# Sparse experts: first-layer weights by a DMA for each tile, the gate's clamp on ScalarE, the norm scale on the turned rows

## The chip, the cores and the metric

The kernel runs on one core of one Trainium2 chip. The metric is the device time of one execution in microseconds (us). A core has five engines with instruction queues of their own: TensorE (PE in the profile; PEld is its loading of weights), VectorE (DVE), ScalarE (ACT), GpSimd (POOL) and SyncE (SP). They meet by semaphores. DMAs are issued from a queue (here SP's, ACT's and GpSimd's) and carried out by 16 DMA engines that all queues share.

## What is computed

Two blocks on x of 16 sequences, 512 tokens, 128 features. The first has a linear recurrence per channel and eight experts of one layer; the second a linear attention with 16 heads and eight experts of two layers, of which each token takes the best two. The change touches only the last of these:

```
def _swiglu(h):
    x_glu = minimum(h[..., ::2], 7.0)
    x_lin = clip(h[..., 1::2], -7.0, 7.0)
    return x_glu * sigmoid(1.702 * x_glu) * (x_lin + 1.0)

t = x * rsqrt(mean(x * x) + EPS) * norm_scale            # 8192 tokens of 128
top_v, top_i = top_k(t @ gate_w + gate_b, 2)
w = zeros.at[token, top_i].set(softmax(top_v))
for w1, b1, w2, b2, we in experts:                       # w1 128x512, w2 256x128
    acc = acc + we * (_swiglu(t @ w1 + b1) @ w2 + b2)
return x + acc
```

## The kernel before

The kernel has three phases. The last, from about 350 us on, holds the second attention, the sparse experts and the sum. Each engine has one block of code in which its instructions stand in their order.

**The attention** goes over 16 sequences (B = 16) in a software pipeline written out by hand: in round n each engine does one step of several sequences. It also norms each sequence's rows, chooses two experts for every token, and scatters each token's row (128 numbers and 4 more, PAY = 132) twice into `rows_of` in DRAM, sorted by expert: `send`, L1479, on GpSimd. At the start of this phase SP loads what the experts need: `w1` of all eight experts (2 MB, L1402) with their biases (L1405) into `w1b1`, which lies in the room of the tile `xg` (so the profile calls it xg), 516 columns for each expert: 512 of weights and 4 of biases. In rounds 7 to 10 ScalarE multiplies the weights by the norm scale `ns`, two experts at a time (`scaled_weights`, L1674). VectorE adds 1 to the biases of the linear half (`numbers`, L1990).

**The plan.** After the last sequence VectorE works out which expert and which rows of `rows_of` each of BT = 72 tiles has (L2036 to L2060). A tile is 256 rows of one expert. The first rows are numbers in `meta`; the experts of 8 tiles are packed into one number in `packs`. An engine loads such a number into a register (`row`, L1335; `packed`, L1340) and takes the expert of a tile out of it by a shift and a mask (`expert`).

**The sparse experts** go over 72 tiles, nine passes of V = 8. For tile v:
- SP loads the 256 rows (132 KB) into slot v % 8 of `xt`, which lies in `kvb` (L1432). It waits until the rows of tile v-8 are turned and their places are worked out.
- TensorE turns the rows (L2417) into bank v % 2. ScalarE copies them to `x_t`, which lies in `qd` (L1725).
- ScalarE copies the expert's 516 columns into `w1c[v % 2]`, which lies in `ex` or `lg` (`own_weights`, L1732). A register gives the column.
- TensorE does the first layer (L2432), 4 matmuls of 128x128 weights with 256 rows, seen as 8 records since fp32 takes two. Their results lie in two banks, gate first.
- VectorE adds the bias and clamps the gate, `glu` (L2104), and the linear half, `lin` (L2109); both lie in `qk`. ScalarE does the gelu of the gate in `gs`, which lies in `nrm` (L1747). VectorE makes the product `act_t`, which lies in `f_t` (L2095).
- Two steps later TensorE adds the bias (L2446) and does the second layer (L2451). ScalarE weighs the result into `yw`, which lies in `h` or `gx` (L1756). Another step later GpSimd scatters it in two DMAs into `parts` in DRAM (L1504).
- For every fourth tile VectorE works out places and weights of four tiles (L2075 to L2088).

The orders are: TensorE turn(v+1), first layer(v), second layer(v-2). ScalarE turned(v+1), own_weights(v+1), gelu(v), weighted(v-2). VectorE gate(v), linear(v), product(v), at times places. After the last tile SP reads `parts` (L1445), VectorE adds it to `x_tok`, and ACT's queue writes the output.

## Time and profile before

| | before |
|---|---|
| runs | 1069.51 us median of 3 (1068.09 to 1073.88) |
| span of the profiled execution | 1003.5 us |
| PE busy | 837.3 us, 83% |
| PEld busy | 645.8 us, 64% |
| DVE busy | 827.6 us, 82% |
| ACT busy | 619.4 us, 62% |
| POOL busy | 563.5 us, 56% |
| DMA | 84.47 MB, mean 84 GB/s |

The span runs from the first to the last instruction; the 66.0 us between it and the median of the runs lie outside. The share of busy time is a mean over stages with different limits. The slices of the page show these (each digit is the busy share in tenths of one fortieth of the span, 25.1 us; PEclk is the clock that TensorE was granted, in tenths of full speed):

```profile
PE   6887972899999579999999999994149999999900
DVE  3987769899997586789999999997638888888848
ACT  3475128899983474587787767746236666666600
POOL 1221018568760534336888888887727676767720
PEclk9999895799999879999999999996569999999955
DMA  5230541333233050000111111111243333233168
```

The last phase starts at slice 15. The sparse experts are slices 30 to 38, the sum is slices 39 and 40.

### The profile page before, as it was taken

Reading aid. Unit: us, or ns where it says so; the run is one execution under the profiler, and the core shown is the slowest. Engines: PE = TensorE matmul, PEld = TensorE weight load, DVE = VectorE, ACT = ScalarE, POOL = GpSimd, SP = SyncE. Lnnn points to the kernel's source line nnn. Section 1 sums busy time; section 2 is a strip of 40 time slices with the busy share of each in tenths; the row PEclk is TensorE's granted clock in tenths of the full one; section 3 lists DMA queues with packets and bytes.
Section 4 is the critical chain, followed back from the end, with each engine's and each line's share of the span. In section 5 each row is a group of like instructions: output and inputs, shape, how many; then the busy total and the mean of one; then the engine's idle time right before and its main releaser. Section 6 shows DMA issues by size and latency. Waiting matters only on the chain.

```text
span 1003.5 us, 22806 instructions
## 1 busy us (share of the span) xinstructions
PE 837.3 (83%) x7439; PEld 645.8 (64%) x7439; DVE 827.6 (82%) x2204; ACT 619.4 (62%) x1669; POOL 563.5 (56%) x573
## 2 busy tenths in 40 slices
PE   6887972899999579999999999994149999999900
PEld 6854652444454268888888888883038888889800
DVE  3987769899997586789999999997638888888848
ACT  3475128899983474587787767746236666666600
POOL 1221018568760534336888888887727676767720
PEclk9999895799999879999999999996569999999955
DMA  5230541333233050000111111111243333233168
GB/s 153 82 90 1 143 134 46 130 105 138 90 127 127 9 145 19 2 10 26 37 44 34 37 36 45 36 37 47 95 122 94 89 90 89 89 95 97 54 227 296
DMA packets 74479, 84.47 MB, mean 84 GB/s; under 512 B 14254, under 2 KB 64361, under 8 KB 72188
## 3 DMA queue, kind: packets, MB, share of 16 engines
q1 hardware_dynamic: 56492, 60.06, 19.7%
q0 software_dynamic: 8704, 18.11, 5.4%
q10 hardware_dynamic: 9168, 4.87, 1.6%
q8 instruction: 61, 1.00, 0.4%
q14 instruction: 54, 0.44, 0.2%
HBM read 59.33 MB, written 23.67 MB: 83 GB/s over the span
## 4 chain that ended last, share of the span: by engine, by line
PE 51%; DVE 6%; DMA 2%; issue 2%; POOL 1%; SPq 1%; ACT 1%; POOLq 0%; DVEq 0%; ACTq 0%
PE ps L2432 13%; PE ps L2194 11%; PE ps L2451 6%; PE ps L2210 3%; PE ps L2272 2%; PE ps L2185 2%; PE ps L2417 2%; PE ps L2331 2%; PE ps L2311 2%; PE ps L2205 1%; POOL rows_of L1479 1%; PE ps L2156 1%; PE ps L2171 1%; PE ps L2259 1%; DVE x_tok L2128 1%
## 5 line engine op out<-in xcount | busy, mean ns | idle before, releaser
L1470 POOL TENSOR_TENSOR kvb<-qk,v 128x1024 f32<-128x1024 f32 x64 | 126.7, 1984 | 74.7 <-DVE qk L1854 50.4
L1479 POOL DMA_INDIRECT rows_of<-payb,posu x128 | 144.1, 1126 | 40.6 <-issue 27.0
L1115 PE MATMUL ps<-masked,ew 128*128 128x512 f32 x256 | 129.9, 623 | 4.2 <-DVE masked L1043 3.5
L2194 PE MATMUL ps<-con,kvb 128*128 128x128 f32 x1024 | 126.0, 276 | 0.0
L2194 PEld LDWEIGHTS ps<-con,kvb 128*128 128x128 f32 x1024 | 119.4, 192 | 1.0 <-issue 1.0
L1504 POOL DMA_INDIRECT parts<-h,dest x72 | 72.8, 1011 | 55.0 <-ACT h L1756 33.3
L1043 DVE TENSOR_TENSOR masked<-f_t,wide 128x512 f32<-128x512 f32 x128 | 88.6, 710 | 9.7 <-PE ps L1115 9.4
L1830 DVE TENSOR_TENSOR qc<-ps,qk 128x1024 f32<-128x1024 f32 x64 | 78.0, 1219 | 17.9 <-PE ps L2194 17.3
L1747 ACT ACTIVATE nrm<-qk 128x512 f32<-128x512 f32 x72 | 45.4, 630 | 72.8 <-DVE qk L2104 72.7
L1504 POOL DMA_INDIRECT parts<-gx,dest x72 | 74.9, 1040 | 25.6 <-issue 23.3
L2451 PE MATMUL ps<-w,f_t 128*128 x576 | 76.1, 275 | 0.0
L2451 PEld LDWEIGHTS ps<-w,f_t 128*128 128x128 f32 x576 | 70.0, 192 | 8.3
L1115 PEld LDWEIGHTS ps<-masked,ew 128*128 128x128 f32 x256 | 43.3, 194 | 47.2 <-issue 23.9
L2432 PE MATMUL ps<-qd,ex 128*128 128x256 f32 x288 | 69.3, 384 | 0.7 <-issue 0.7
L2432 PE MATMUL ps<-qd,lg 128*128 128x256 f32 x288 | 68.3, 380 | 0.3 <-issue 0.3
L2432 PEld LDWEIGHTS ps<-qd,ex 128*128 128x128 f32 x288 | 52.8, 193 | 6.8 <-ACT qd L1725 0.9
L2432 PEld LDWEIGHTS ps<-qd,lg 128*128 128x128 f32 x288 | 51.9, 190 | 6.2 <-issue 0.5
L891 ACT ACTIVATE junk<-x_tok,stat 128x128 f32<-128x128 f32 x128 | 49.4, 387 | 10.4 <-DVE stat L1019 9.8
L2095 DVE SCALAR_TENSOR_TENSOR f_t<-qk,nrm 128x512 f32<-128x512 f32 x72 | 50.5, 701 | 6.4
L2104 DVE TENSOR_SCALAR qk<-ps,ex 128x256 f32<-128x256 f32 x72 | 31.5, 478 | 29.3 <-PE ps L2432 29.3
L2417 PE MATMUL ps<-con,kvb 128*128 128x128 f32 x144 | 28.1, 277 | 25.1 <-DMA kvb<-rows_of 25.1
L2104 DVE TENSOR_SCALAR qk<-ps,lg 128x256 f32<-128x256 f32 x72 | 31.5, 478 | 8.1 <-PE ps L2432 8.0
(354 smaller groups left out, 2237.7 us busy)
## 6 DMA issues: line engine op xcount, KB each, us to landing
wide<-hot_dram SPq DMA_DIRECT2D x16, 1024.0 KB, 4.6
kvb<-rows_of SPq DMA_DIRECT2D x72, 132.0 KB, 2.1
toep<-taps_dram SPq DMA_DIRECT2D x16, 512.0 KB, 6.1
x_tok<-in_x_dram SPq DMA_DIRECT2D x16, 256.0 KB, 3.1
out_dram<-x_tok ACTq DMA_DIRECT2D x16, 256.0 KB, 5.6
rows<-rows_dram SPq DMA_DIRECT2D x16, 192.0 KB, 3.2
kvb<-parts SPq DMA_DIRECT2D x6, 512.0 KB, 6.9
rows<-rows_dram SPq DMA_DIRECT2D x16, 128.0 KB, 4.5
```

Source lines behind the costliest of these rows:

```text
L891: last = nc.scalar.activation(junk[j][:, c, :], source(t), ACT.Square, bias=total[:, t:t + 1], scale=float(D), accum_out=out_sq[:, t:t + 1])
L1043: nc.vector.tensor_tensor(masked[e % 4][:, :], f_t[w % W][:, :], wide[w % W][:, e, :], ALU.mult).then_inc(s["masked"], 1)
L1115: nc.tensor.matmul(ps[:, w % 2, :], ew0[:, e, :], masked[e % 4][:, :], start=False, stop=(e == E - 1)).then_inc(s["product"], 1)
L1470: nc.gpsimd.tensor_tensor(kv[g % KB][:, :, :].rearrange("p e (h d) -> p e h d", h=H), k_in, v_in, ALU.mult).then_inc(s["kv"], 1)
L1479: nc.gpsimd.indirect_dma_start(rows_of, bass.IndirectOffsetOnAxis(ap=posu[w % 2][:, slot, t:t + 1], axis=0), pay[w % PB][:, t, :], None).t ...
L1504: nc.gpsimd.indirect_dma_start(parts, bass.IndirectOffsetOnAxis(ap=dest[:, u, c:c + 1], axis=0), yw[u][:, c, :], None).then_inc(s_out[u], 16)
L1830: nc.vector.tensor_tensor(qc[g % 2][:, :, :], cum(g), q_in, ALU.mult).then_inc(s["qc"], 1)
L2095: nc.vector.scalar_tensor_tensor(act_t[v % 2][:, :, :], lin[v % 2][:, :, :], -6.0, gs[v % 2][:, :, :], ALU.max, ALU.mult).then_inc(m["a"], 1)
L2104: last = nc.vector.tensor_scalar(glu[v % 2][:, f, :], ps[:, bank, f * SP:(f + 1) * SP], w1c[v % 2][:, I2 + f:I2 + f + 1], 7.0, ALU.add, AL ...
L2194: last = nc.tensor.matmul(cum(g)[:, e, :], kv[g % KB][:, e, :], k("upto"), start=True, stop=True)
L2432: last = nc.tensor.matmul(ps[:, bank + f // 2, (f % 2) * SP:(f % 2 + 1) * SP], w1c[v % 2][:, f * P:(f + 1) * P], x_t[v % 2][:, :], start=T ...
L2451: last = nc.tensor.matmul(to, act_t[v % 2][:, j, c * P:(c + 1) * P], w2[:, bass.ds(e * (2 * D) + j * D, D)], start=False, stop=(c == S - 1 ...
```

## The change

1. **Weights by DMA.** The 2 MB load of `w1` at the start of the phase goes. SP issues after the row load of each tile a DMA of this tile's expert from DRAM, 128 x 512 numbers (256 KB, pieces of 2 KB), with the expert from a register as part of the address. It goes to one of WC = 4 buffers, the halves of `ex` and `lg`, and waits until the first layer of tile v-4 is done. TensorE waits for its landing (`s_w1`). `own_weights` goes. The biases get a tile of their own, `b1`; ScalarE and VectorE take the column of a tile by a register.
2. **ScalarE clamps the gate.** As min(h + b, 7) = 7 - relu(7 - b - h), ScalarE does a Relu with scale -1 and bias 7 - b on each half of the gate, and the gelu gets scale -1 and bias 7. VectorE no longer reads the gate. `hg_ps` is new: TensorE signals after the second of four matmuls, so that the gate can begin. TensorE also waits until the gate of tile v-2 is read. `numbers` prepares 7 - b by two operations more.
3. **Norm scale.** `scaled_weights` goes; the scale is an operand of the activation that copies the turned rows.
4. The packed numbers are loaded ahead on ScalarE and VectorE, and at the start of each pass on SP. SP waits before its first tile for three more semaphores of the attention, since `ex` and `lg` are now written by DMA.

```diff
@@ SyncE, at the start of the phase
-                    by_expert = w1b1.rearrange("p (e i) -> p e i", i=WB)
-                    sp.dma_start(by_expert[:, :, 0:I2], a["w1"]).then_inc(s["experts"], 16)
@@ SyncE, the sparse experts
+                    need(sp, "sub", B)
+                    need(sp, "ln", B)
+                    need(sp, "qk", B)
+
                     def body(t, steps):
+                        packed = t.packed() if t.exists(0) else None
                         for v in steps:
                             at = t.row(v)
                             t.done("x_ps", v - V, alone=True)
                             t.grouped("dest", v - V, alone=True)
                             sp.dma_start(xt[:, v, :, :], rows_of[bass.ds(at, SP), :].rearrange("(p c) d -> p c d", c=S)).then_inc(s_in[v], 16)
+                            e = t.expert(packed, v)
+                            t.done("h_ps", v - WC)
+                            sp.dma_start(w1c[v % WC], a["w1"][:, bass.ds(e, 1), :].rearrange("p e i -> p (e i)")).then_inc(s_w1[v % WC], 16)
@@ ScalarE
-                        if 5 <= n - 2 <= 8:
-                            scaled_weights(n - 2 - 5)
...
-                            nc.scalar.activation(x_t[v % 2][:, :], ps[:, v % 2, 0:SP], ACT.Copy).then_inc(m["x_t"], 1)
-
-                    def own_weights(t, packed, v):
-                        if t.exists(v):
-                            e = t.expert(packed, v % V)
-                            t.done("h_ps", v - 2)
-                            t.done("lin", v - 2)
-                            nc.scalar.activation(w1c[v % 2][:, :], w1b1[:, bass.ds(e * WB, WB)], ACT.Copy).then_inc(m["w1c"], 1)
+                            nc.scalar.activation(x_t[v % 2][:, :], ps[:, v % 2, 0:SP], ACT.Copy, scale=ns[:, :]).then_inc(m["x_t"], 1)
...
                             turned(t, v + 1)
-                            own_weights(t, packed if v + 1 < V else following, v + 1)
                             if t.exists(v):
+                                e = t.expert(packed, v)
+                                bank = 2 + 2 * (v % 2)
+                                t.done("hg_ps", v)
+                                for f in range(2):
+                                    last = nc.scalar.activation(glu[v % 2][:, f, :], ps[:, bank, f * SP:(f + 1) * SP], ACT.Relu,
+                                                                bias=b1[:, bass.ds(e * NF + f, 1)], scale=-1.0)
+                                last.then_inc(m["glu"], 1)
                                 t.done("a", v - 2)
                                 t.done("glu", v)
-                                nc.scalar.activation(gs[v % 2][:, :, :], glu[v % 2][:, :, :], ACT.Gelu_apprx_sigmoid).then_inc(m["gs"], 1)
+                                nc.scalar.activation(gs[v % 2][:, :, :], glu[v % 2][:, :, :], ACT.Gelu_apprx_sigmoid, bias=limit[:, :], scale=-1.0).then_inc(m["gs"], 1)
@@ VectorE
-                                t.done("gs", v - 2)
                                 t.done("h_ps", v)
-                                for f in range(2):
-                                    last = nc.vector.tensor_scalar(glu[v % 2][:, f, :], ps[:, bank, f * SP:(f + 1) * SP], w1c[v % 2][:, I2 + f:I2 + f + 1], 7.0,
-                                                                   ALU.add, ALU.min)
-                                last.then_inc(m["glu"], 1)
@@ TensorE
                                 t.done("x_t", v)
-                                t.done("w1c", v)
+                                if t.exists(v):
+                                    wait(pe, s_w1[v % WC], 16 * ((t.i * V + v) // WC + 1))
                                 t.done("lin", v - 2)
+                                t.done("glu", v - 2)
                                 for f in range(NF):
-                                    last = nc.tensor.matmul(ps[:, bank + f // 2, (f % 2) * SP:(f % 2 + 1) * SP], w1c[v % 2][:, f * P:(f + 1) * P], x_t[v % 2][:, :],
+                                    last = nc.tensor.matmul(ps[:, bank + f // 2, (f % 2) * SP:(f % 2 + 1) * SP], w1c[v % WC][:, f * P:(f + 1) * P], x_t[v % 2][:, :],
                                                             start=True, stop=True)
+                                    if f == 1:
+                                        last.then_inc(m["hg_ps"], 1)
                                 last.then_inc(m["h_ps"], 1)
```

## Rows read from the trace of the kernel before

**Rows 1.** Windows by stretch: busy us (x instructions) by engine, clock, DMA share, GB/s

```profile
core 0: us, PE busy (x) PEld busy (x) DVE busy (x) ACT busy (x) POOL busy (x), PEclk, DMA share, GB/s
364.00:368.00 4.00, 3.84 (x16) 3.62 (x17) 2.92 (x5) 0.79 (x3) 3.91 (x3) 0.57 1.05 403
...
490.00:510.00 20.00, 20.00 (x218) 16.95 (x217) 18.80 (x52) 16.23 (x43) 17.11 (x13) 1.00 0.14 39
...
800.00:840.00 40.00, 40.00 (x258) 35.95 (x258) 34.81 (x93) 26.79 (x70) 27.76 (x28) 1.00 0.30 88
```

**Rows 2.** Timeline of PE, one expert tile: start us, us, [idle before <-releaser]

```profile
800.03 0.38 PE L2417 MATMUL ps<-con,kvb 128*128 128x128 f32 x2
800.25 1.89 PE L2432 MATMUL ps<-qd,ex 128*128 128x256 f32 x8
...
802.09 1.06 PE L2451 MATMUL ps<-w,f_t 128*128 x8
802.98 0.38 PE L2417 MATMUL ps<-con,kvb 128*128 128x128 f32 x2
```

**Rows 3.** Timeline of ACT in the same tile: gelu and weighted result

```profile
800.27 0.63 ACT L1747 ACTIVATE nrm<-qk 128x512 f32<-128x512 f32 x1 [1.01 <-DVE qk L2104]
800.81 0.61 ACT L1756 ACTIVATE h<-ps,own 128x128 f32<-128x128 f32 x2
```

**Rows 4.** Groups by line, 760 to 900 us: busy us, mean ns | idle before

```profile
L1504 POOL DMA_INDIRECT parts<-gx,dest x48 | 50.2, 1046 | 17.6 <-issue 16.3 <-ACT gx L1756 1.3
...
L2104 DVE TENSOR_SCALAR qk<-ps,ex 128x256 f32<-128x256 f32 x48 | 21.0, 478 | 6.1 <-PE ps L2432 6.1
...
L1725 ACT ACTIVATE qd<-ps 128x256 f32<-128x256 f32 x48 | 18.3, 382 | 0.0
```

**Rows 5.** The tile ns: the scaling in the attention, ns min/median/max, first and last start

```profile
L1674 ACT ACTIVATE xg<-xg,ns x4: 1139/1142/1145, 444.2 to 505.2; 128x1024 f32<-128x1024 f32 x4
```

**Rows 6.** Timeline of PE: first layers of tiles 0 to 3

```profile
740.77 2.96 PE L2432 MATMUL ps<-qd,ex 128*128 128x256 f32 x8
...
743.78 1.89 PE L2432 MATMUL ps<-qd,lg 128*128 128x256 f32 x8
...
746.57 1.97 PE L2432 MATMUL ps<-qd,ex 128*128 128x256 f32 x8 [0.67 <-issue]
...
750.03 1.32 PE L2432 MATMUL ps<-qd,lg 128*128 128x256 f32 x5 [0.27 <-issue]
```

**Rows 7.** Timeline of ACT in the same stretch

```profile
741.94 1.28 ACT L1747 ACT_TABLE_LOAD   x1
744.78 0.63 ACT L1747 ACTIVATE nrm<-qk 128x512 f32<-128x512 f32 x1 [1.56 <-DVE qk L2104]
...
749.30 0.63 ACT L1732 ACTIVATE lg<-xg 128x516 f32 x1 [0.16 <-issue]
```

**Rows 8.** SP's timeline, its number load, and DMA issues: KB, us to landing

```profile
737.05 8.07 SPq L1432 DMA_DIRECT2D kvb<-rows_of  x8
...
L1335 SPq TENSOR_LOAD <-meta x72: 263/271/401, 736.3 to 927.1; - x72
...
kvb<-rows_of SPq DMA_DIRECT2D x72, 132.0 KB, 2.1
x_tok<-in_x_dram SPq DMA_DIRECT2D x16, 256.0 KB, 3.1
...
xg<-in_w_dram SPq DMA_DIRECT2D x1, 2048.0 KB, 10.2
```

**Rows 9.** Timeline of POOL and ACT, end of the expert stage

```profile
949.05 0.61 ACT L1756 ACTIVATE h<-ps,own 128x128 f32<-128x128 f32 x2
...
950.44 0.96 POOL L1504 DMA_INDIRECT parts<-h,dest  x1 [1.31 <-ACT h L1756]
...
955.55 0.96 POOL L1504 DMA_INDIRECT parts<-gx,dest  x1 [0.36 <-ACT gx L1756]
...
961.85 0.96 POOL L1504 DMA_INDIRECT parts<-gx,dest  x1 [0.30 <-DMA parts<-gx,dest]
```

More of the change, by code:

```diff
@@ L1157, in build @@
         NF = I2 // P
[L1158 to L1160 removed]
+        room = xg[:, :, :].rearrange("p d t -> p (d t)")
         V = 8
@@ L1256, in build @@
                      "pay", "pay_ps", "pay_t", "gx", "x4", "lg_ps", "lg_t", "lg_back", "lg", "max", "idx", "idf", "hot", "ed", "ee", "e1", "p1", "taken", "counted", "carried",
-                     "rank_ps", "rank", "sel", "pos", "posu", "extra", "labels", "totals", "base", "place", "pads", "experts", "plan", "padrow", "beside", "scaled")
+                     "rank_ps", "rank", "sel", "pos", "posu", "extra", "labels", "totals", "base", "place", "pads", "experts", "plan", "padrow", "beside")
             s = {nm: sem(f"p3_{nm}") for nm in names}
@@ L1274, in build @@
             b2x = sb("b2x", [P, E * D], BF16, scope=sc)
-            b2f, b2r = (room[0:3, E * WB + q * E * D:E * WB + (q + 1) * E * D] for q in range(2))
+            b2f, b2r = (room[0:3, q * E * D:(q + 1) * E * D] for q in range(2))
             b2h = sb("b2h", [3, E * D], BF16, scope=sc)
@@ L1279, in build @@
             x_t = [qd[:, v * SP:(v + 1) * SP] for v in range(2)]
-            w1c = [q[:, :, :].rearrange("p j t -> p (j t)")[:, 0:WB] for q in (ex, lg)]
+            WC = 4
+            w1c = [(ex, lg)[j // 2][:, j % 2, :] for j in range(WC)]
+            b1 = sb("b1", [P, E * NF], scope=sc)
+            limit = sb("limit", [P, 1], scope=sc)
+            s_w1 = [sem(f"p4_weights{j}") for j in range(WC)]
             glu = [qk[0][:, v, :].rearrange("p (f t) -> p f t", f=2) for v in range(2)]
@@ L1418, in _ @@
                     sp.wait_ge(s["pads"], 16 * E)
-                    sp.wait_ge(s["experts"], (2 + NF) * 16)
+                    sp.wait_ge(s["experts"], (1 + NF) * 16)
                     for j in range(PB):
@@ L1438, in _ @@
                         sp.wait_ge(s_in[v], 16 * NP)
+                    for j in range(WC):
+                        sp.wait_ge(s_w1[j], 16 * (BT // WC))
                     for v in range(V):
@@ L1668, in logits_kept @@
                             nc.scalar.activation(lg_t[:, :], ps[:, LOGIT, 0:P], ACT.Copy).then_inc(s["lg_t"], 1)
-                    def scaled_weights(q):
-                        need(act, "experts", (2 + NF) * 16)
-                        act.wait_ge(s["weights"], 3 * 16)
-                        by_e = w1b1.rearrange("p (e i) -> p e i", i=WB)[:, 2 * q:2 * q + 2, 0:I2]
-                        nc.scalar.activation(by_e, by_e, ACT.Copy, scale=ns[:, :]).then_inc(s["scaled"], 1)
                     def turned_pay(w):
@@ L1714, in _ @@
                     act.wait_ge(s["place"], 2)
-                    need(act, "scaled", E // 2)
+                    act.wait_ge(s["weights"], 3 * 16)
                     need(act, "den", B)
@@ L1734, in body @@
+                    ahead = [act.value_load(packs[0:1, 0:1], min_val=0, max_val=E ** V - 1)]
                     def body(t, steps):
-                        first = isinstance(t.i, int) and t.i == 0
-                        packed = t.packed() if t.exists(0) else None
-                        following = None
+                        packed = ahead.pop() if ahead else None
                         for v in steps:
-                            if v == 0 and first:
-                                own_weights(t, packed, 0)
+                            if v == 0 and isinstance(t.i, int) and t.i == 0:
```

26 lines of the change are left out of this document (16 added, 10 removed).

## The prediction

> **What bounds the kernel now.** I read the page's slices first: TensorE (PE) stands at nine tenths or more from slice 16 to 27 (the second attention) and from slice 31 to 38 (the sparse experts), and low between them and at the end. The windows by stretch say it more sharply: 20.00 of 20 us in 490 to 510 us and 40.00 of 40 us in 800 to 840 us, both at a granted clock of 1.00, which is 2.4 GHz; ScalarE (ACT) has 16.23 and 26.79 us there [rows 1]. The change touches the experts above all, so I then read the order of one of the 72 tiles on TensorE: the turning of the rows starts at 800.03, the first layer at 800.25, the second layer at 802.09, and the next turning at 802.98 us [rows 2]. One tile takes 2.95 us, and no idle time stands before any of these groups. The first layer and the bias matmul behind it fill the 1.84 us from 800.25 to 802.09, the second layer 0.89 us, the turning 0.22 us: nothing is left over. TensorE is not waiting for anybody: it streams.
>
> The question of every part below is therefore whether it touches that stream, or one of its two ends. The rest of an expert tile, per tile: ScalarE 0.38 (turned rows) + 0.63 (copy of the weights) + 0.63 (gelu) + 0.61 (weighted result) = 2.25 us [rows 3, 4, 7]; VectorE (DVE) two clamps of the gate, two of the linear half and the product, all in all 34.81/40 x 2.95 = 2.57 us [rows 1]; GpSimd (POOL) two scatters of 1.05 us with 0.30 us before each, 2.7 us [rows 4, 9].
>
> **Part 1: the copy of the weights goes, and ScalarE takes the clamp of the gate.** ScalarE loses 0.63 us a tile and gains two activations of 128x256 out of PSUM. It has such a shape already, the turned rows: 0.382 us alone, and two activations that follow each other overlap (the two of 128x128 of the weighted result take 0.61 together) [rows 3, 4]; so 0.64 to 0.76 us. ScalarE goes from 2.25 to at most 2.38 us, under 2.95. VectorE loses two clamps of 0.478 us [rows 4] and gains a few register operations: 2.57 to about 1.7 us. No engine but TensorE was at its limit, so both together are worth 0 in the 72 tiles while TensorE streams.
>
> What covers it, and with what room? I laid the new order against one step of 2.95 us that starts with the turning. The first half of the first layer ends near 0.22 + 0.86 = 1.1 us, so the gate's clamp runs 1.2 to 1.9, the gelu to 2.5; the linear half follows the end of the first layer near 2.1 and is done at 3.0; the product ends near 3.7. The second layer of that tile starts two steps later, at 5.90 + 2.05 = 8.0 us. The new wait on TensorE, that the gate of two tiles ago has been read, is satisfied 4 us early; behind it in TensorE's queue stand the first layer and all that follows, so it would cost its full lateness, but it has 4 us. The new wait on ScalarE for the first half of the layer stands ahead of the gelu and the weighted result of tile v-2. That result's matmuls end at 0.15 us of the next step, and today ScalarE reaches it only at 800.81, 0.78 us into the step, since the gelu before it ends late [rows 3]. In the new order ScalarE is free by then. So GpSimd gets its work some 0.5 us earlier in each tile. In the middle of the stage that is worth nothing.
>
> **Part 2: the weights come by DMA, 256 KB for each tile.** SyncE (SP) issues them between the row loads. Eight row loads with an address from a register took 8.07 us, 1.0 to 1.1 us each [rows 8]; the second DMA of a tile needs a shift and a mask in place of the load of a number, so at most another 1.1 us: 2.2 of 2.95 us at the most, and SyncE keeps up. The row loads are now queued behind the wait of the weights: they leave 3 tiles ahead in place of 7 or 8, and VectorE, which wants four tiles' rows at every fourth tile, still has them over 4 us early. The weights of tile v leave at the end of the first layer of v-4, and are wanted 4 x 2.95 - 1.9 = 9.9 us later. For their landing the trace has two bounds: the row load of 132 KB with 2.1 us and the load of 256 KB with 3.1 us [rows 8]. I take 2.6 to 3.1, as the size is that of the second, and the worst single load of the stage before, 2 MB, took 10.2 us [rows 8]. Room of 6.8 us or more, four buffers deep: cost 0. The traffic: 262144 B in 2.95 us is 89 GB/s on top of 88 in this stage, while 403 GB/s have been moved in 364 to 368 us [rows 1]. It fits twice over.
>
> The Trainium skill (DMA: Bandwidth & Descriptors, Anatomy of one DMA) fits a DMA's time as about 2.0 us plus its bytes over 436e3 per us, 2.6 us for 256 KB, an estimate by that page; it was measured for GpSimd's path, and the rows here (2.1 and 3.1 us) lie on either side of it. By the page the first tile would have its weights 0.5 us sooner than by the upper row, and the sum below would end 0.3 us lower.
>
> **Part 3: the scaling leaves the attention stage.** Four activations of 1.142 us [rows 5], 4.57 us of ScalarE, go. They lie between 444 and 505 us where TensorE is at 20.00 of 20 [rows 1]. Value 0; bounds -0.5 (TensorE's only gap nearby is some tenths) and +0.2. The norm scale on the turned rows is the scale operand of an activation that is there anyway: 0. The 2 MB load at 359 us goes too; nobody waits on it before 441 us, where VectorE gets two more tiny operations of under 0.2 us: 0.
>
> **Part 4: the start of the expert stage.** Here the chain is a latency. SyncE must, after the last scatter, read the packed expert numbers (the load of a number takes 0.27 us [rows 8], with the register operations behind it some 0.6 us, over half of what one issue takes) and pass three more waits before the first row load: about +0.75 us. The weights of tile 0 leave 0.6 us after that, near 738.5, and land near 741.3 to 741.6. Today the first layer starts at 740.77; new near 741.5, by both paths alike. It runs at the slow clock (2.96 us in place of 1.89 [rows 6]), so tile 1 starts near 744.5 in place of 743.78. Then two stalls of today go: tile 2 waited (0.67 us before it) for rows that ScalarE turned only after the gelu of tile 0 at 744.78, and tile 3 waited 0.27 us for its copied weights at 749.30 to 749.93 [rows 6, 7]. New: clamp of tile 0 while its layer ends, table load of 1.28 us (today hidden under the wait at 741.94 [rows 7]), gelu, turned rows of tile 2 near 745.9, so tile 2 near 746.6 against 746.57, tile 3 near 749.65 against 750.03. Sum of the start: -0.4 us; bounds -0.7 (weights at 2.6 us) and +1.5 (all the delay stays).
>
> **Part 5: the end of the stage.** GpSimd's last ten scatters follow each other at 1.26 us from 950.44 on, where it had waited 1.31 us for ScalarE's result of 949.05, and the last starts at 961.85 [rows 9]. That result could start at 948.0, as its matmuls are done then. The chain moves ahead by 1.1 us at its head, but at the fifth scatter (955.55) meets the result of tile 69, which comes only 0.5 to 0.6 sooner. I take -0.6; bounds -1.1 and +0.3.
>
> **The sum**: 0 (72 tiles) + 0 (attention, -0.5 to +0.2) - 0.4 (-0.7 to +1.5) - 0.6 (-1.1 to +0.3) = -1.0 us, bounds -2.3 to +2.0. It is made against the profiled span of 1003.5 us, which becomes 1002.5. The runs have a median of 1069.51 us, 66.0 more than the span, and nothing of the change lies outside it: 1069.5 - 1.0 = 1068.5 us. What a measurement of this kernel tells from no change is about 0.5%, 5.3 us; the three runs of before lie 5.8 us apart.
>
> **Rivals.**
> (a) *ScalarE in truth holds the attention stage.* Then 4.57 us come off there, and with the lower bounds of start and end (-0.7 - 1.1) it is -6.4, 1063 us. For it: ScalarE is in many chains there. Against it: 20.00 of 20 us on TensorE in the very stretch. Chance 0.07.
> (b) *The weights land late.* Four buffers: four steps = landing + first layer 1.9 + 0.4 us. It decides from a landing of 9.5 us. At the 10.2 us of the 2 MB load a step is 3.12 us, +0.17 x 68 = +12 us: 1080. Against it: 3.1 us for this size. Chance 0.04.
> (c) *GpSimd becomes the bound.* Two scatters of 1.05 + 0.30 us make 2.7 of 2.95 us [rows 4]. The scatters share the DMA engines with twice the traffic. If one takes over 1.175 us the stage goes by GpSimd: at 1.3 us the step is 3.2, +0.25 x 72 = +18 us: 1087. Against it: the median is lower than the mean, and most of its work is to write descriptors. Chance 0.04.
> (d) *ScalarE changes its table twice a tile.* Relu and the gelu would be in different tables, 2 x 1.283 us [rows 7]: ScalarE at 2.38 + 2.57 = 4.95 us a tile, +2.0 x 72 = +144: 1213 us. For it: no row shows a Relu beside this gelu. Against it: the turned rows' Copy stands beside it today with one load in the stage. Chance 0.02. The Trainium skill (ScalarE: Activation LUTs, Table sets: the hidden batching unit) says that cheap functions like relu and copy are in every set; by that rule (d) doesn't exist.
> (e) *The start costs more than its bounds, or the waits add a gap per tile*: 0.07 us on each of 72 steps is +5. The waits are handled ahead of the stream, so 0.02.
>
> **How the numbers follow.** The forecast has 0.81 and is within 0.5% by its bounds. Faster is (a), 0.07. Slower is (b) to (e), 0.12. The forecast's own range is 1067 to 1072; the spread of the runs of before (-1.4 and +4.4 about their median) widens it to 1064 to 1075, which together holds eight in ten; (a) lies just under its lower end, and (b) to (d) far above its upper one.
>
> **What would show it.** In the changed kernel's profile: the turnings 2.95 us apart in the middle of the stage and no idle time before the first layer (wrong if a DMA or ScalarE stands there as releaser); weights landing in 2.5 to 3.5 us; one table load; GpSimd's wait for ScalarE shorter; VectorE near 60% of the stage; attention windows at 20 of 20; first layer of tile 0 some 0.7 us later after the first row load's old place, of tile 3 a little earlier. A DMA share over 0.8 or scatters over 1.17 us would make it wrong.

## The result, and the profile after

The changed kernel takes 1071.26 us (median of 20 runs, 1069.35 to 1075.07) against 1068.38 us of the kernel before beside it (20 runs, 1060.66 to 1073.88): ratio 1.0033, interval 1.0019 to 1.0046. That is 3.5 us slower by the ratio (2.9 by the two medians), inside the 0.5% that count as no change, but on the other side of the -1.0 us forecast. Its profiled execution has a span of 1069.8 us. The page's head, and the slices of TensorE, VectorE, ScalarE and GpSimd:

```profile
span 1069.8 us, 23451 instructions
...
PE 850.0 (79%) x7424; PEld 650.8 (61%) x7439; DVE 770.8 (72%) x2062; ACT 648.3 (61%) x1737; POOL 551.7 (52%) x573
...
PE   6887935999996699999999999630588888888810
...
DVE  4897778899986767899999999762454544545448
ACT  3574248899943756768777766360466766667510
POOL 1310047477724344378888888757055555555520
```

TensorE has an 8 in slices 30 to 38, where the forecast wanted 9. The windows by stretch (columns as in [rows 1]) say it in us:

```profile
490.00:510.00 20.00, 19.72 (x214) 16.60 (x214) 18.40 (x52) 15.00 (x39) 16.62 (x13) 1.00 0.12 39
800.00:840.00 40.00, 33.48 (x207) 28.77 (x205) 20.56 (x59) 27.25 (x70) 21.01 (x22) 1.00 0.49 143
840.00:880.00 40.00, 34.66 (x218) 29.95 (x216) 18.67 (x50) 26.07 (x66) 21.08 (x23) 1.00 0.51 152
```

33.48 of 40 us in place of 40.00 [rows 1], at the same granted clock of 1.00: TensorE waits 16% of a stage that the prediction took for a stream. VectorE has fallen to 20.56 us, so the clamps are gone as meant. Who stands ahead of the idle time, from the waits of 780 to 1000 us (us in total, times, longest):

```profile
DVE f_t L2098 <- PE ps L2460: 61.4, 24, 3.0
...
POOL parts L1514 <- ACT h L1756: 37.6, 15, 4.0
POOL parts L1514 <- ACT gx L1756: 35.1, 15, 2.6
...
PE ps L2439 <- ACT qd L1727: 32.0, 30, 2.1
ACT gx L1756 <- PE ps L2460: 29.4, 13, 2.3
ACT h L1756 <- PE ps L2460: 25.3, 11, 3.6
```

No DMA is named: the weights are in time. TensorE waits for ScalarE's turned rows, GpSimd for ScalarE's weighted results, and both VectorE's product (L2098) and ScalarE's weighted result (L1756) for TensorE's signal that a second layer (L2460) is done.

Two tiles of the stage, engine after engine: GpSimd, ScalarE, VectorE, TensorE.

```profile
845.17 0.95 POOL L1514 DMA_INDIRECT parts<-gx,dest  x1 [2.45 <-ACT gx L1756]
846.43 0.96 POOL L1514 DMA_INDIRECT parts<-gx,dest  x1 [0.30 <-issue]
847.70 0.95 POOL L1514 DMA_INDIRECT parts<-gx,dest  x1 [0.30 <-issue]
848.96 0.96 POOL L1514 DMA_INDIRECT parts<-gx,dest  x1 [0.31 <-issue]
852.49 0.96 POOL L1514 DMA_INDIRECT parts<-gx,dest  x1 [2.58 <-ACT gx L1756]
```

```profile
843.76 0.62 ACT L1756 ACTIVATE gx<-ps,own 128x128 f32<-128x128 f32 x2 [2.13 <-PE ps L2460]
...
846.20 0.61 ACT L1756 ACTIVATE gx<-ps,own 128x128 f32<-128x128 f32 x2
...
848.00 0.72 ACT L1747 ACTIVATE nrm<-qk,limit 128x512 f32<-128x512 f32 x1
851.03 0.68 ACT L1756 ACTIVATE gx<-ps,own 128x128 f32<-128x128 f32 x2 [2.31 <-PE ps L2460]
851.60 0.47 ACT L1727 ACTIVATE qd<-ps,ns 128x256 f32<-128x256 f32 x1
```

```profile
847.08 0.86 DVE L2112 TENSOR_SCALAR qk<-ps,b 128x256 f32<-128x256 f32 x2
850.94 0.69 DVE L2098 SCALAR_TENSOR_TENSOR f_t<-qk,nrm 128x512 f32<-128x512 f32 x1 [3.00 <-PE ps L2460]
```

```profile
844.80 1.99 PE L2439 MATMUL ps<-qd,ex 128*128 128x256 f32 x8 [0.96 <-ACT qd L1727]
...
846.74 1.06 PE L2460 MATMUL ps<-w,f_t 128*128 x8
...
847.85 1.89 PE L2439 MATMUL ps<-qd,ex 128*128 128x256 f32 x8
...
852.12 1.99 PE L2439 MATMUL ps<-qd,lg 128*128 128x256 f32 x8 [1.16 <-ACT qd L1727]
```

The product at 850.94 is that of tile 24, whose first layer is the group of 844.80. It needs its linear half (done 847.94), its gelu (848.00 + 0.72 = 848.72) and the second layer of tile 22, which is the group of 846.74, ended at 847.80. By these rows all of it is there at 848.72, and it starts 2.2 us later. ScalarE's weighted result of tile 22 starts at 851.03, 2.3 us after ScalarE came free. Both go on together, 2.0 us after GpSimd's fourth scatter in a row began (848.96).

What is late is TensorE's signal. The trace also records when a semaphore is raised, though no row prints it. The signal of tile 22's second layer is recorded at 850.92, 3.1 us after the end of its matmuls and 0.02 us before the product starts. Five more signals of TensorE follow within 0.31 us, for groups of matmuls that started between 847.63 and 850.59, so TensorE worked on while its signals stood still. (The ends of matmuls are modelled, their starts are recorded.)

The turned rows that stand behind the weighted result in ScalarE's queue come at 851.60, and TensorE waits 1.16 us for them. So it goes on from pair to pair: two first layers 3.05 us apart, the next 4.3. The four scatters stand in a row because the two weighted results of a pair (843.76 and 846.20) come 2.44 us apart, and GpSimd needs 2 x 1.26 = 2.52 us for one.

Two measures from the trace's rows make this countable in every kernel. **Late products**: of tiles 2 to 71, those that start over 1 us after the last of gelu and second layer they need (the normal distance is 0.13 to 0.15 us). **Groups of scatters**: scatters that start under 1.35 us after the one before them. The changed kernel has 30 late products, and 23 groups of four beside 14 of two. The recorded trace of before has no late product. In 25 of the 30 (28 of 30 and all 10 in new profiles of the two kernels, a_again and b_again below) the signal of the second layer is recorded 0.02 us before the late start. The recorded signals that ScalarE and VectorE send in this stage are never over 0.04 us behind their own operations, in any of nine profiles with scatters. Up to two thirds of the signals of one kind have no record there, so the rest is not known.

### The profile page after: what moved, and what is told of

The parts are those of the page before. It is cut to its first block, busy times and chain, and to the rows that moved or that the text cites. A ratio compares the mean times of both kernels' runs of the same rounds, so it can differ in the third digit from the quotient of the medians.

```text
span 1069.8 us, 23451 instructions
## 1 busy us (share of the span) xinstructions
PE 850.0 (79%) x7424; PEld 650.8 (61%) x7439; DVE 770.8 (72%) x2062; ACT 648.3 (61%) x1737; POOL 551.7 (52%) x573
## 3 DMA queue, kind: packets, MB, share of 16 engines
q8 instruction: 62, 1.02, 0.4%
## 4 chain that ended last, share of the span: by engine, by line
PE 47%; DVE 7%; ACT 4%; issue 3%; another core or an unknown queue 3%; DMA 1%; SPq 1%; ACTq 0%; POOL 0%; DVEq 0%; POOLq 0%
PE ps L2439 12%; PE ps L2199 10%; PE ps L2460 6%; PE ps L2215 3%; PE ps L2190 2%; PE ps L2277 2%; PE ps L2264 2%; PE ps L2161 1%; ACT qd L1727 1%; PE ps L2210 1%; PE ps L2316 1%; PE ps L2176 1%; PE ps L2422 1%; DVE x_tok L2133 1%
## 5 line engine op out<-in xcount | busy, mean ns | idle before, releaser
L2098 DVE SCALAR_TENSOR_TENSOR f_t<-qk,nrm 128x512 f32<-128x512 f32 x72 | 50.7, 704 | 106.9 <-PE ps L2460 64.3
L2199 PE MATMUL ps<-con,kvb 128*128 128x128 f32 x1024 | 127.3, 278 | 0.0
L1514 POOL DMA_INDIRECT parts<-h,dest x72 | 69.4, 964 | 83.1 <-ACT h L1756 64.5
L1514 POOL DMA_INDIRECT parts<-gx,dest x72 | 69.1, 960 | 59.4 <-ACT gx L1756 39.8
L1830 DVE TENSOR_TENSOR qc<-ps,qk 128x1024 f32<-128x1024 f32 x64 | 77.9, 1217 | 18.5 <-PE ps L2199 18.4
L2439 PE MATMUL ps<-qd,ex 128*128 128x256 f32 x288 | 71.8, 393 | 15.9 <-ACT qd L1727 15.9
L2112 DVE TENSOR_SCALAR qk<-ps,b 128x256 f32<-128x256 f32 x144 | 62.8, 477 | 26.6 <-PE ps L2439 17.0
L2460 PE MATMUL ps<-w,f_t 128*128 x576 | 77.7, 278 | 0.2 <-issue 0.2
L2460 PEld LDWEIGHTS ps<-w,f_t 128*128 128x128 f32 x576 | 71.2, 195 | 8.4
L1742 ACT ACTIVATE qk<-ps,b 128x256 f32<-128x256 f32 x144 | 60.7, 483 | 9.1 <-remote 5.3
L1747 ACT ACTIVATE nrm<-qk,limit 128x512 f32<-128x512 f32 x72 | 52.0, 722 | 7.2 <-issue 0.4
L1727 ACT ACTIVATE qd<-ps,ns 128x256 f32<-128x256 f32 x72 | 34.0, 472 | 36.6 <-PE ps L2422 34.8
```

Of the source, the lines that this page charges most:

```text
L1514: nc.gpsimd.indirect_dma_start(parts, bass.IndirectOffsetOnAxis(ap=dest[:, u, c:c + 1], axis=0), yw[u][:, c, :], None).then_inc(s_out[u], 16)
L1742: last = nc.scalar.activation(glu[v % 2][:, f, :], ps[:, bank, f * SP:(f + 1) * SP], ACT.Relu, bias=b1[:, bass.ds(e * NF + f, 1)], scale=-1.0)
L1747: nc.scalar.activation(gs[v % 2][:, :, :], glu[v % 2][:, :, :], ACT.Gelu_apprx_sigmoid, bias=limit[:, :], scale=-1.0).then_inc(m["gs"], 1)
L1830: nc.vector.tensor_tensor(qc[g % 2][:, :, :], cum(g), q_in, ALU.mult).then_inc(s["qc"], 1)
L2112: last = nc.vector.tensor_scalar(lin[v % 2][:, f, :], ps[:, bank + 1, f * SP:(f + 1) * SP], b1[:, bass.ds(e * NF + 2 + f, 1)], 8.0, ALU.ad ...
L2199: last = nc.tensor.matmul(cum(g)[:, e, :], kv[g % KB][:, e, :], k("upto"), start=True, stop=True)
```

## The experiments

Each ratio is to the kernel before on the same chip. All the measures stand in one table at the end of this section.

### Is the recorded trace of before like its timed executions?

b_again is the kernel before and a_again the changed one, unchanged.

> The kernel before, unchanged, with a new trace. If the recorded trace (span 1003.5 us) stands for the timed runs (1068 us), the new span is within 5 us of 1003.5 and the expert tiles are 2.95 us apart. If instead the recorded trace is an execution that went faster than the timed ones, the new span is near 1066 us, and the 60 us lie somewhere that the two traces of the same code can show: tiles further apart than 2.95 us, a longer way from the attention to the experts, or a clock.

> The changed kernel, unchanged, with a new trace on the same chip as the kernel before. If its span of 1069.8 us stands for it: 1068 to 1073 us again, expert tiles about 3.5 us apart. If its trace too can differ from execution to execution, the span moves by tens of us.

Measured: 1069.6 us, ratio 1.002 [0.9993, 1.0048], and 1072.34 us, ratio 1.0031 [1.0005, 1.0058]. The new profile of before has a span of **1063.0 us, not 1003.5**. Its windows, its last scatter of the attention, and SyncE's first row loads and register operations:

```profile
800.00:840.00 40.00, 35.87 (x225) 31.28 (x225) 29.71 (x82) 23.39 (x60) 23.46 (x24) 1.00 0.26 77
840.00:880.00 40.00, 35.28 (x215) 30.77 (x214) 29.15 (x82) 22.59 (x57) 23.68 (x23) 0.96 0.26 76
```

```profile
747.90 0.95 POOL L1479 DMA_INDIRECT rows_of<-payb,posu  x1 [0.30 <-issue]
```

```profile
758.37 8.49 SPq L1432 DMA_DIRECT2D kvb<-rows_of  x8
```

```profile
L1335 SPq TENSOR_LOAD <-meta x72: 3/267/709, 757.6 to 980.5; - x72
L1335 SPq FUSED_REGOPS  x72: 3/152/727, 757.9 to 980.8; - x72
```

The kernel before has TensorE at 35.87 of 40 us as well, and 10 late products. Of the 59.5 us between its two profiles, 38.2 lie from the first turned rows to the first addition of the sum (229.3 in the recorded trace, 267.5 here) and 21.3 ahead of that: 14.7 in the attention rounds up to the last activation of L1618 (2.8 of them by the eleventh, so most where the rounds end), the rest behind it, where 10.5 us lie from the last scatter to the first row load (747.90 to 758.37) in place of 3.4. SyncE's number load, at most 401 ns in [rows 8], takes up to 709. The timed runs agree with the new trace: each run's time is its span plus 1.7 to 3.6 us. So next to nothing of the 66 us lies outside the span; the recorded trace is of an execution without pauses that the timed ones have. From here on both kernels are compared by their new profiles.

### Are GpSimd's scatters the source, and does the sum hold without them?

x3 is before and x4 after with the 144 scatters of the expert stage replaced by 72 plain DMAs on ScalarE's queue, to fixed rows (left out: that each token's results go to the token's own place).

```diff
-    nc.gpsimd.indirect_dma_start(parts, bass.IndirectOffsetOnAxis(ap=dest[:, u, c:c + 1], axis=0), yw[u][:, c, :], None)
+    act.dma_start(parts[at:at + SP, :].rearrange("(p c) d -> p c d", c=S), yw[u][:, :, :])
```

> The kernel before with GpSimd's 144 scatters of the expert stage replaced by 72 plain DMAs of the same bytes on ScalarE's queue to fixed rows (it leaves out where the results belong, so the sum is of other rows). Theory (GpSimd's scatters hold back every engine's answers): tiles are 2.95 us apart, as in the recorded trace of before, and the stage is 30 to 38 us shorter, about 1033 us. Rival (DMA traffic or something of this execution as a whole holds the answers back): the tiles stay at 3.4 us, 1066 us.

> The same replacement in the changed kernel (it too leaves out where the results belong). Theory: without the scatters my forecast for the change holds, the tiles are 2.95 us apart and it is within 3 us of the kernel before with the same replacement. Rival (the change has a cost of its own, by DMA or by ScalarE, without any scatter): tiles over 3.0 us apart or 5 us and more behind.

Measured: 1017.45 us (0.9577 [0.9527, 0.9627]) and 1016.36 us (0.9567): the changed kernel is **1.1 us faster**, each pair of runs within 0.3 us. Windows of x4, and its DMA issues (KB, us to landing):

```profile
800.00:840.00 40.00, 40.00 (x261) 35.98 (x261) 24.37 (x65) 34.60 (x82) 0.00 (x0) 1.00 0.60 179
840.00:880.00 40.00, 40.00 (x256) 35.83 (x256) 25.05 (x72) 34.17 (x82) 0.00 (x0) 1.00 0.63 183
```

```profile
ex<-in_w_dram SPq DMA_DIRECT2D x36, 256.0 KB, 2.9
lg<-in_w_dram SPq DMA_DIRECT2D x36, 256.0 KB, 3.0
```

The stream is back, 40.00 of 40 us, 2.95 us a tile, with more DMA traffic than any other kernel here has in this stage (179 GB/s), no late product, and the weights landing in 2.9 to 3.0 us. With plain DMAs in place of the scatters before takes 1060.75 - 1017.45 = 43 us less, and the change goes from +3.5 to -1.1 us (two runs of each kernel). DMA traffic of this size costs nothing that shows. TensorE's signals agree: in x3, x4 and the recorded trace all 72 signals of the second layer are recorded 0.01 to 0.02 us behind the end of its matmuls.

### Which part of the change?

x1 is before with the clamp of the gate on ScalarE and nothing else; x2 is after with the clamp back on VectorE.

```diff
 (x1, in before: ScalarE takes the clamp; VectorE's two clamps go)
+    nc.scalar.activation(glu[v % 2][:, f, :], ps[:, bank, f * SP:(f + 1) * SP], ACT.Relu, bias=w1c[v % 2][:, I2 + f:I2 + f + 1], scale=-1.0)
 (x2, in after: ScalarE's go)
+    nc.vector.tensor_scalar(glu[v % 2][:, f, :], ps[:, bank, f * SP:(f + 1) * SP], b1[:, bass.ds(e * NF + f, 1)], 7.0, ALU.add, ALU.min)
```

> The kernel before with one part of the change alone: ScalarE clamps the gate by a Relu, VectorE no longer; the copy of the weights on ScalarE and the scaling in the attention stay. Theory (ScalarE's place in the tile's loop): the expert stage is held by answers that come late while GpSimd scatters, and with the clamp on ScalarE its queue gelu, weighted result, turned rows is in the loop with more work, so this part alone costs more than the whole change, 1074 to 1080 us. Rival (weights' traffic): the clamp is free and this kernel stands at 1066 to 1069 us like the one before; the loss comes from the 256 KB of every tile.

> The changed kernel with its clamp put back on VectorE: weights by a DMA for each tile, no copy on ScalarE, norm scale on the turned rows. Theory: ScalarE has 0.64 us a tile less in the loop, so it is at or below the kernel before, 1058 to 1068 us. Rival (traffic): the DMAs slow the answers further, and it is as slow as the changed kernel or slower, 1071 to 1078 us.

Measured: x1 1052.95 us, 0.992 [0.9892, 0.9948]; x2 1060.84 us, 0.9995 [0.9972, 1.0019]. I had expected x1 to be slower, and it is 8 us faster. The clamp gains 0.8% where ScalarE also copies the weights. Where the weights come by DMA no gain is left: x2, without the clamp, has 0.9995, and the changed kernel 1.0033, 1.0031 and (r_after, below) 1.0007 on other chips. That the clamp loses there is not shown. Neither part by itself is slower than before. In x1 ScalarE has 0.38 + 0.64 + 0.85 + 0.72 + 0.61 = 3.2 us for each tile, over 2.95, and the scatters come in groups of two (58 of 61). In the changed kernel it has 2.65 us, and they come in fours. That gave theory A: an emptier ScalarE catches up after a pause, delivers two weighted results 2.4 us apart, under the 2 x 1.26 us that GpSimd needs for one, and so makes a group of four, which holds ScalarE and VectorE for longer (by the signals above: which holds back TensorE's signals for longer). The link from groups of four to the time is argued, not shown.

### Put the copy back, cut the traffic, space the scatters, take the scale alone

```diff
 (x5, after: an unneeded ScalarE copy of 128x516 for each tile)
     turned(t, v + 1)
+    nc.scalar.activation(idle[:, 1, :], idle[:, 0, :], ACT.Copy)
 (x6, after: 64 of 512 columns of the weights)
+    sp.dma_start(w1c[v % WC][:, 0:I2 // 8], a["w1"][:, bass.ds(e, 1), 0:I2 // 8]...)
 (x7, after, GpSimd, ahead of the scatters of tile v-3)
+    t.done("h_ps", v - 1)
 (x8, x1 with the norm scale on the turned rows; scaled_weights gone)
+    nc.scalar.activation(x_t[v % 2][:, :], ps[:, v % 2, 0:SP], ACT.Copy, scale=ns[:, :])
```

> The changed kernel with a ScalarE copy of 128x516 fp32 put back between the turned rows and the clamp of each tile; what it copies is not used, the weights still come by DMA. ScalarE has 0.63 us more to do for each tile. Theory A (order of the queues: with ScalarE emptier the weighted results of two tiles come close together, GpSimd issues its scatters in bursts of four in place of two, ScalarE and VectorE stand still until 2 us after each burst): the copy works as a spacer, the bursts go back to two and the time falls to that of the clamp alone, ratio 0.990 to 0.996. Theory B (the second DMA of each tile, with its traffic, is what costs): nothing changes, 1.003. Theory C (ScalarE is simply too full in these executions): +0.63 x 72 x about a half = +20 us, ratio 1.02.

> The changed kernel with the weights' DMA cut to the first 64 of 512 columns (32 KB in place of 256 KB for each tile; seven eighths of the first-layer weights are left out, so the first layer multiplies by what stands in the buffer). The count of DMAs and every wait stay. Theory B (the traffic of the weights slows the scatters and holds their landing back): ratio falls from 1.003 to that of the clamp alone, 0.990 to 0.996. Theory A (order of the queues) and theory C (ScalarE): no change, 1.001 to 1.006, bursts of four scatters as before.

> The changed kernel with one more wait on GpSimd: the two scatters of tile v-3 also wait for the first layer of tile v-1. Nothing else changes. Theory A (bursts of four scatters hold ScalarE and VectorE): bursts of four become rarer than 23 of 41, and the time falls by 5 to 15 us, ratio 0.990 to 0.998. Theories B and C: the wait is either met already (ratio 1.003) or delays the scatters (up to 1.01).

> The kernel before with the clamp of the gate on ScalarE and the norm scale on the turned rows, the scaling in the attention stage gone; the weights are still copied by ScalarE, no DMA. Against the clamp alone (0.992) this takes 4.57 us of ScalarE out of the attention and adds about 0.09 us for each turned-rows activation. All theories: attention unchanged within 1 us. Theory A: expert stage about as with the clamp alone, ratio 0.989 to 0.996. Theory C (ScalarE full): +0.09 x 72 = +6 us, 0.998. If the scale operand is what spoils the changed kernel: 1.00 or more.

Measured: x5 1054.52 us, **0.9957** [0.9928, 0.9986]; x6 1058.81 us, 1.0015 [0.9981, 1.0049]; x7 1061.41 us, 1.0008 [0.9983, 1.0034]; x8 1048.72 us, 0.9896 [0.9842, 0.995]. Work that nobody needs makes the changed kernel faster: for theory A, against a full ScalarE (theory C, 1.02 expected). An eighth of the bytes moves it little (the interval still allows 0.5% either way), so theory B, the traffic, does not explain the 1.1% between x1 and the changed kernel. The wait of x7 was a miss. Its profile has GpSimd wait for a first layer six times, 10.3 us in all, but 16 groups of four were left, and the time shows no gain, so x7 says nothing for or against theory A. The scale operand costs nothing that shows.

### On one chip: the copy, a gap in GpSimd's queue, fixed biases

x10 clears 128x512 numbers of an unused buffer on GpSimd after each tile's scatters; x11 takes the biases from a fixed column (left out: the choice of the expert's bias), so ScalarE and VectorE do no register operations.

```diff
 (x10)
+    pool.wait_ge(s_idle, t.i * V + v - LAG)
+    nc.gpsimd.memset(idle, 0.0).then_inc(s_idle, 1)
 (x11; on VectorE b1[:, 2 + f:3 + f])
-    bias=b1[:, bass.ds(e * NF + f, 1)]
+    bias=b1[:, f:f + 1]
```

> The changed kernel as it is, on the chip of the three runs below: ratio 1.001 to 1.005 by its earlier comparisons on other chips, bursts of four scatters. Every theory says the same; it is the base of the other three.

> The changed kernel with the unneeded ScalarE copy, beside the changed kernel on one chip. Theory A (bursts): 0.993 to 0.998, which is 5 to 10 us under r_after, bursts of two. If the earlier 0.9957 was the chip and not the copy: as r_after, 1.001 to 1.005.

> The changed kernel; GpSimd clears 128x512 numbers of an unused buffer (about 0.52 us) after the two scatters of each tile. Theory A1 (what counts is the length of an unbroken burst: ScalarE and VectorE go on in any gap): bursts of two, 0.990 to 0.998. Theory A2 (the gap has to let GpSimd run out of scatters, since the hold lasts 2 us after the last one in any case): GpSimd has 0.5 us more to do for each tile and is now the bound with 2 x 1.26 + 0.5 = 3.0 us plus the hold, ratio 1.003 to 1.02.

> The changed kernel with the biases of the first layer taken from a fixed column, so that ScalarE and VectorE read no packed expert numbers and do no register operations (the choice of the expert's bias is left out). If register operations, held at 0.7 us each as SyncE's are, spoil the changed kernel: 0.990 to 0.997. Theory A: no change, 1.001 to 1.005, or worse, as ScalarE is emptier still.

Measured: r_after 1061.18 us, 1.0007 [0.9978, 1.0036]; r_copy 1057.49 us, 0.9974 [0.995, 0.9997]; x10 1056.35 us, 0.9949 [0.9925, 0.9972]; x11 1059.04 us, 0.998 [0.9953, 1.0008]. Against r_after the copy takes off 3.7 us (0.4 to 7.3, resampling the 12 runs of each), the clearing 4.8 (2.2 to 8.1); the fixed biases 2.1, with an interval from -0.7 to 5.6, so their part stays open. The interval of r_after allows no loss at all as well as the 0.3% of the result. GpSimd in r_copy, same stretch as above:

```profile
840.32 0.96 POOL L1516 DMA_INDIRECT parts<-gx,dest  x1 [0.72 <-ACT gx L1760]
841.58 0.96 POOL L1516 DMA_INDIRECT parts<-gx,dest  x1 [0.30 <-issue]
843.27 0.96 POOL L1516 DMA_INDIRECT parts<-gx,dest  x1 [0.72 <-issue]
844.53 0.96 POOL L1516 DMA_INDIRECT parts<-gx,dest  x1 [0.30 <-issue]
847.72 0.96 POOL L1516 DMA_INDIRECT parts<-h,dest  x1 [2.23 <-ACT h L1760]
```

Between the pairs there are now 0.7 us, and the profile has one group of four in place of 19 and 4 late products in place of 21; it is the profile of the fastest of the twelve runs. Its record of the second layer's signals is complete: 29 of 72 still come over 1 us late, up to 3.8 us. So shorter groups don't do away with the late signals.

### Is it the groups of four, or does the clearing help anyhow?

x12 is before and x13 is x8, each with the clearing of x10; x14 is x8 again.

> The kernel before, with GpSimd clearing 128x512 numbers of an unused buffer after the two scatters of each tile, as in x10. Theory A (the clearing cuts bursts of four; the kernel before has nearly none, 59 of its 62 are of two): no gain, ratio 0.999 to 1.003. Rival (the clearing helps whatever the bursts are): 0.993 to 0.997, as it took 0.0058 off the changed kernel.

> The kernel of x8 (clamp on ScalarE, copy kept, norm scale on the turned rows) with the same clearing on GpSimd. Its bursts are of two in 61 of 63. Theory A: as x14 below, within 0.003. Rival: 0.005 under x14.

> The kernel of x8 again, with more rounds: 0.9896 with an interval of 0.984 to 0.995 so far. If it holds, 0.988 to 0.993, faster than both kernels.

Measured: x12 1063.69 us, 0.9966 [0.9943, 0.9989]; x13 1060.98 us, 0.993 [0.9904, 0.9956]; x14 1059.72 us, 0.9928 [0.9898, 0.9958]. x13 went as theory A says, x12 did not: the clearing helps the kernel before, which has one group of four. So x10 is no proof of theory A, and why a pause between pairs helps there too is open. What stands on its own is the copy: it touches neither GpSimd nor the count of scatters, and it gained on two chips. x14 confirms that the clamp on ScalarE with the copy kept and the scale moved (x8) is faster than the kernel before, by 0.7%, and so than the changed one.

All kernels, from the profiled execution of each. The last column is the sum of the pauses of over 1.4 us in which neither ScalarE nor VectorE starts an operation, in us, from the fifth turned rows to the fourth from last:

```
kernel          ratio    groups of 2 / 4   late products   common pauses
recorded before   -        46 /  7              0                0
b_again         1.002      59 /  1             10               33
x3, x4          0.957       no scatters         0                0
a_again         1.0031      6 / 26             30               83
after           1.0033     14 / 23             30               75
r_after         1.0007     21 / 19             21               73
x7_spaced       1.0008     24 / 16             26               70
x6_small        1.0015     26 / 17             28               67
x11_fixed_bias  0.998      16 / 19             14               61
x2_dma          0.9995     37 / 12              9               50
x10_pool_gap    0.9949     63 /  0              9               46
x12_before_gap  0.9966     63 /  0              6               27
r_copy          0.9974     55 /  1              4               25
x8, x14         0.99       61 /  0         15, 10           27, 20
x1_clamp        0.992      58 /  1             13               19
x5_copy_back    0.9957     59 /  0              6               16
x13_best_gap    0.993      63 /  0             13               14
```

All kernels with 16 or more groups of four have a ratio of 0.998 or more and over 60 us of common pauses; those with at most one and a lighter VectorE have 0.998 or less and under 50. The recorded trace has 7 groups of four and no pause at all: a group is not enough, the execution has to be one that pauses. Each row is one execution, and not always a typical one: that of x12 is 4.3 us under its kernel's median, that of x13 4.4 us above. Nor does the time follow the late products alone: x1 has 13 at 0.992, x2 has 9 at 0.9995.

## Why the prediction was wrong, point by point

**The step that failed: the sum was made against the recorded span of 1003.5 us, and "the 66.0 between it and the median of the runs lie outside the span"**. All but 1.7 to 3.6 us of them lie inside the timed executions' span: 1063.0 in b_again, and 1069.8 in the changed kernel. The term that this made wrong is the "0 (72 tiles)", which Part 1 gives "while TensorE streams". It does not stream: the tiles are 3.47 us apart in b_again and 3.60 in a_again, in place of 2.95, and tiles 3 to 71 take 235.7 us in the one and 243.7 in the other. (The runs' medians differ by 2.7 us, less than these two executions; b_again's was 3.5 us under its kernel's median.) Everything that was costed at nothing because TensorE streams (40.00 of 40) was costed in an execution that none of the new profiles resembles; in b_again TensorE has 35.87 of 40 us, and ScalarE, VectorE and GpSimd are in the chain. The gap of 66 us was in the text and was explained away; only 1.7 to 3.6 us lie outside a span.

**Where the premise holds, the zero of the tiles holds.** Without the scatters tiles 3 to 71 take 200.6 us in x3 and 200.4 in x4, 2.95 a tile, which supports the zero of the 72 tiles and Part 2. The whole, x4 against x3, is -1.1 us by the medians and -1.0 by the spans, forecast -1.0, but that agreement is luck: of the 1.0 us, 0.5 lie ahead of the attention's last scatter (forecast 0), nothing from there to tile 3 (forecast -0.4), 0.2 in the tiles and 0.2 behind them (forecast -0.6, from a chain of GpSimd that is gone in both).

**Part 1, ScalarE and VectorE.** The prices were low, as the rows had no activation of these shapes with a scale or bias taken from a tile. The clamp pair takes 0.83 to 0.85 us (0.64 to 0.76 taken), the turned rows with a scale operand 0.47 (0.38), the gelu with a bias operand 0.72 (0.63). 0.47 + 0.85 + 0.72 + 0.61 = 2.65 us a tile against "at most 2.38"; x4 has 34.60/40 x 2.95 = 2.55. Still under 2.95, so this error alone cost nothing. VectorE: 24.37/40 x 2.95 = 1.80, forecast 1.7. Part 1's second failed sentence is here: GpSimd gets its work 0.5 us earlier in each tile, and "in the middle of the stage that is worth nothing". With the copy gone as well, the results of two tiles come within 2.4 us of each other, and groups of two become groups of four; with the copy kept (x1) they stay groups of two, and with the copy gone and the clamp on VectorE (x2) 12 of four appear. That the longer groups are what costs the time is theory A, and not shown.

**Part 2, the weights.** Right: 2.9 to 3.0 us to land, taken 2.6 to 3.1, and no wait for them. The 2.6 us estimated from the Trainium skill (DMA: Bandwidth & Descriptors, Anatomy of one DMA) is 0.3 to 0.4 us short of what x4 shows.

**Part 3, the attention.** Right: x3 and x4 reach the last activation of that stage (L1618 of before) at 701.4 and 701.3 us, so 4.57 us of ScalarE were worth 0.1 in these two executions. Nothing speaks for rival (a).

**Part 4, the start.** The -0.4 is not borne out: in x3 and x4 the first layer of tile 0 comes 8.5 and 9.9 us after the attention's last scatter (+1.4, forecast +0.7), and that of tile 3 18.4 us after it in both. With the scatters a sum of tenths can't be read at all: from the last scatter to the first row load SyncE needs 10.5 us in b_again and 9.7 in the changed kernel, in place of 3.4. The table load came once, after the first clamp, as forecast:

```profile
763.92 0.84 ACT L1742 ACTIVATE qk<-ps,b 128x256 f32<-128x256 f32 x2 [1.42 <-PE ps L2439]
764.78 1.28 ACT L1747 ACT_TABLE_LOAD   x1
766.07 0.72 ACT L1747 ACTIVATE nrm<-qk,limit 128x512 f32<-128x512 f32 x1
```

**Part 5, the end.** In the changed kernel GpSimd's last fourteen scatters stand in groups of six and eight with 4.64 us of waiting for ScalarE between them, so the -0.6 was not there to be had. From the last first layer to the end of the span it is 56.9 us, against 55.2 in b_again:

```profile
1013.60 0.95 POOL L1514 DMA_INDIRECT parts<-h,dest  x1 [0.30 <-issue]
1019.19 0.95 POOL L1514 DMA_INDIRECT parts<-gx,dest  x1 [4.64 <-ACT gx L1756]
```

**The rivals.** (b), (c) and (d) did not come: weights in 3 us, one scatter at 0.96 us on average (less than before's 1.05), one table load. (e), a gap per tile by waits, is the nearest: there is a gap per pair of tiles, but its waits end with late signals of TensorE, which are there in b_again too, without the new waits. The range held the time since 0.3% is little, not since the working was right.

## What to carry to other kernels

Where the profiled span and the median of the runs are 66 us apart, take a second profile before costing anything: "TensorE is at 40 of 40, so the rest is free" is true only of the execution it was read from. Where GpSimd issues scatters, an engine made emptier can make the kernel slower (here the ScalarE copy, put back, took off 3.7 us, interval 0.4 to 7.3). Longer unbroken groups of scatters are the likely link, not a shown one, so look at the spacing of the scatters before and after, and at when the awaited signal is recorded, not only at the end of the operation that sends it. Of two edits that belong together, try each alone: here the clamp with the copy kept gains 0.7 to 1%, and with the DMA in the copy's place that gain is gone.

## What the runs showed of the hardware

While GpSimd issues DMA_INDIRECTs 1.26 us apart, TensorE's signals often arrive late, and ScalarE and VectorE, which wait for them, stand still although the rows show all their inputs as done. In the changed kernel's profile signals that belong to matmuls up to 3 us apart arrive in a bunch, within 0.31 us. Behind a group of four the two engines mostly go on 1.9 to 2.0 us after its last one began. The delays tend to come in steps: in the three profiles of the changed kernel and in x6 and x11, 154 of 350 products start 0.1 to 0.3 us after their last input, and most of the others pile up near 0.75 (34 at 0.7 to 0.9), 1.45 (16 at 1.4 to 1.6) and 2.2 us (60 at 2.1 to 2.3), roughly 0.13 plus one, two and three times 0.7; 34 more lie at 0.4 to 0.7, between the steps. SyncE's small steps show the same 0.7 us: its number load takes up to 709 ns in place of 267, its register operations up to 727 in place of 152. With the scatters gone the late products and late signals are gone too. Late products are in every new profile of a kernel with scatters and nowhere in the recorded one. Which part of a scatter does it (writing descriptors, the semaphores, the writes of single rows to DRAM), and why that one execution was spared, was not tried.

The Trainium skill (SBUF — State Buffer, SBUF: two separate sides) says that among the engines contention for SBUF is on a port pair shared by VectorE and GpSimd alone, and that TensorE and ScalarE never wait at theirs. The first half would fit one row: scatters took 1.02 to 1.03 us on average in the kernels with the gate's clamp on VectorE (before, b_again, x2, x12), 0.96 to 0.98 in those without; whether the port is the reason no run tells. The second half is not contradicted. It speaks of ports, and what ScalarE waits for here, together with VectorE, is a signal of TensorE.
